# Turning the gathered rows of an expert layer by DMA transposes instead of matmul-engine transposes, from slot 3 on

## What is computed

```python
xn = _layernorm(x, axis=-1)
s = _L0_attn_ref(xn, Wqkv, b_qkv, Wout, b_out)        # attention, (8, 512, 512)
# the feed-forward layer: each token takes the one expert that its router picks
h = jnp.einsum('nd,ehd->enh', x_flat, w_fc)            # 512 -> 2048
a = jnp.square(jnp.where(h >= 0, h, 0.5 * h))
expert_out = jnp.einsum('enh,edh->end', a, w_proj)     # 2048 -> 512
out = jnp.einsum('end,en->nd', expert_out, mask * top_weight[None, :])
g = _silu(out)
x = x + s * g
```

## Time and profile before

| | before |
|---|---|
| median of 3 runs | 1480.56 us (1479.88 to 1480.98) |
| the profiled execution | 1481.51 us, of which the span from first to last instruction is 1479.7 us |
| PE busy | 1384.0 us (94%) |
| DVE, ACT, POOL busy | 923.9, 770.7, 682.5 us |
| DMA, mean | 90 GB/s |

### The profile page before, as it was taken

How to read it: one execution, slowest core, us unless ns; L and a number is a source line. 1 busy time by engine, 2 the same in 40 slices (tenths; PEclk the granted TensorE clock), 3 DMA queues, 4 the chain that set the end, 5 groups by cost and what they waited for, 6 DMA issues and landing times.

```text
span 1479.7 us, 30039 instructions
## 1 busy us (share of the span) xinstructions
PE 1384.0 (94%) x9863; PEld 880.8 (60%) x9863; DVE 923.9 (62%) x2441; ACT 770.7 (52%) x1824; POOL 682.5 (46%) x896
## 2 busy tenths in 40 slices
PE   2889999999999999999689999999999999999995
PEld 1455555655555565555456666666666666666663
DVE  7577777777777777777759745555444555544444
ACT  3478778787777878787736422222222222222221
POOL 0356667465666746566523433333333333323332
PEclk9989999999999999999999999999999999999998
DMA  4425334343534434245346311110011111010100
GB/s 161 144 86 148 125 115 125 110 139 100 171 101 130 128 106 138 89 141 140 107 164 207 115 44 44 44 43 25 23 41 42 39 44 44 30 29 30 36 30 30
DMA packets 84897, 133.45 MB, mean 90 GB/s; under 512 B 14095, under 2 KB 63247, under 8 KB 82576
## 3 DMA queue, kind: packets, MB, share of 16 engines
q1 hardware_dynamic: 75808, 105.70, 23.0%
q0 software_dynamic: 8944, 25.83, 5.6%
HBM read 97.81 MB, written 33.95 MB: 89 GB/s over the span
## 4 chain that ended last, share of the span: by engine, by line
PE 75%; DVE 10%; POOL 6%; ACT 3%; issue 3%; DMA 1%; DVEq 1%; SPq 0%; ACTq 0%; POOLq 0%
PE psY L1126 19%; PE psF L1106 19%; PE psA L352 19%; PE psT L446 7%; PE psA L461 5%; POOL pr L941 4%; PE psS L425 3%; DVE sg L1303 2%; PE psX L1080 1%; POOL route L969 1%; PE psA L409 1%; DVE stat L749 1%; DVE am L636 1%; ACT stage L519 1%; DVE wf L1225 1%
## 5 line engine op out<-in xcount | busy, mean ns | idle before, releaser
L1106 PE MATMUL psF<-xT,wf 128*128 128x256 f16 (+1 forms) x3264 | 368.0, 269 | 0.0
L1126 PE MATMUL psY<-wf,aT 128*128 x1584 | 363.9, 379 | 0.3 <-DVE aT L1270 0.3
L1106 PEld LDWEIGHTS psF<-xT,wf 128*128 x3264 | 312.0, 98 | 63.5
L1344 POOL TENSOR_TENSOR a<-a 128x512 f32<-128x512 f32 (+1 forms) x136 | 153.1, 1126 | 392.1 <-DVE a L1261 390.5
L941 POOL TENSOR_SCALAR pr<-pr,rden 128x128 f32<-128x128 f32 (+3 forms) x512 | 268.4, 542 | 141.9 <-DVE rden L868 140.3
L579 ACT ACTIVATE pr<-pr,mn 128x128 f32<-128x128 f32 (+3 forms) x512 | 281.9, 553 | 0.0
L857 DVE CUSTOM_DVE_ANT_0 pr<-psS,base,nsl 128x128 f32<-128x128 f32 (+3 forms) x512 | 249.6, 543 | 4.2 <-PE psS L425 4.2
L1126 PEld LDWEIGHTS psY<-wf,aT 128*128 128x128 f16 x1584 | 154.5, 98 | 158.5 <-issue 1.0
L446 PE MATMUL psT<-conf,pr 128*128 128x128 f32 x1280 | 205.7, 279 | 18.1 <-POOL pr L941 16.5
L1183 ACT ACTIVATE rl<-psF 128x512 f32<-128x512 f32 (+1 forms) x136 | 79.3, 583 | 263.2 <-PE psF L1106 263.0
L446 PEld LDWEIGHTS psT<-conf,pr 128*128 128x128 f32 x1280 | 157.3, 143 | 81.3 <-POOL pr L941 27.3
(11 more groups left out here) (155 smaller groups left out, 1371.0 us busy)
## 6 DMA issues: line engine op xcount, KB each, us to landing
qk_parts<-pre SPq DMA_DIRECT2D x64, 256.0 KB, 2.8
qs<-qk_parts SPq DMA_DIRECT2D x128, 128.0 KB, 2.7
ks<-qk_parts SPq DMA_DIRECT2D x128, 128.0 KB, 2.7
wst<-in_wf SPq DMA_DIRECT2D x16, 1024.0 KB
wstage<-in_wf SPq DMA_DIRECT2D x32, 512.0 KB, 4.6
xin<-in_x SPq DMA_DIRECT2D x32, 256.0 KB, 4.4
attn_out<-so SPq DMA_DIRECT2D x32, 256.0 KB, 2.0
pt<-in_wqkv SPq DMA_DIRECT2D x4, 768.0 KB, 10.1
```

The costliest lines, as they stand in the source:

```text
L1106: last = nc.tensor.matmul(psF[c % 2][:, k * TT:k * TT + tn], w(e, 2 * hc, hl, kc * 512 + col, P), xT[:, r % 2, x, kc, 0:tn], start=(m == 0 ...
L1126: last = nc.tensor.matmul(psY[r % 2][h][:], aT[:, c % 4, x, k, h * P:(h + 1) * P], w(e, 2 * hc + 1, hl, q * 512, 512), start=(c == 0 and k ...
L1344: nc.gpsimd.tensor_tensor(at, at, at, ALU.mult).then_inc(s["a_ready"], 1)
```

## The change

The rows of slots 3 to 16 are no longer turned by PE. ACT and DVE split the normalised half into its high and low parts token by token, into a new view `xs` of the staging ring (free once the weights are in), and SP then issues eight DMA transposes for each half: two parts by four blocks of 128 by 128 float16, each from `xs` in SBUF to `xT` in SBUF. The first `up` of such a slot waits for the semaphores of these DMAs. Slots 0 to 2 are turned as before. SP issues the transposes in a loop that stands behind all its other work.

```diff
@@ att_sync
         for i in range(QB):
             sp.wait_ge(s_out[i], 16 * (B + 1))
+        ffn["turn"](sp)
@@
+BY_DMA = 3
@@ ffn_block
+    xs = wstage[:, 0, :].bitcast(F16).rearrange("p (h x d) -> p h x d", h=NH, x=2)
+    turned_in = [sem(f"turned_in{i}") for i in range(NH)]
@@
+    def turn(sp):
+        for n in range(BY_DMA, SLOTS):
+            for h in range(halves(n)):
+                sp.wait_ge(s["X_lo"], n * NH + h + 1)
+                sp.wait_ge(s["F_done"], (n - 1) * GR)
+                for x in range(2):
+                    for kc in range(KC):
+                        sp.dma_start_transpose(xT[:, n % 2, x, kc, h * P:(h + 1) * P],
+                                               xs[:, h, x, kc * P:(kc + 1) * P]).then_inc(turned_in[h], 16)
+
+    def rows_turned(eng, n, h):
+        eng.wait_ge(turned_in[h], (n - BY_DMA + 1) * 2 * KC * 16)
@@ up
-            if c == 0:
+            if c == 0 and n < BY_DMA:
                 wait(pe, s["X_lo"], n * NH + halves(n))
+            if c == 0 and n >= BY_DMA:
+                for h in range(halves(n)):
+                    rows_turned(pe, n, h)
@@ step of PE
-                if c in (1, 3) and n >= 0 and ahead and (c - 1) // 2 < halves(n + 1):
+                if c in (1, 3) and n >= 0 and ahead and n + 1 < BY_DMA:
                     xtrans(pe, n + 1, (c - 1) // 2)
@@ turn_hi
+        if n >= BY_DMA:
+            act.wait_ge(s["ln_done"], n * NH + h + 1)
+            if n == BY_DMA:
+                act.wait_ge(s["ws_lo"], len(order))
+            else:
+                rows_turned(act, n - 1, h)
+            nc.scalar.activation(xs[:, h, 0, :], xn[:], ACT.Copy, scale=1024.0).then_inc(s["X_hi"], 1)
+            return
@@ norm
-        wait(dve, s["X_done"], n * NH + h)
+        k = n * NH + h
+        wait(dve, s["X_done"], min(k, BY_DMA * NH))
+        if k > BY_DMA * NH:
+            dve.wait_ge(s["X_hi"], k)
+            dve.wait_ge(s["X_lo"], k)
@@ turn_lo
+        if n >= BY_DMA:
+            stt(out=xs[:, h, 1, :], in0=xn[:], scalar=1024.0, in1=xs[:, h, 0, :],
+                op0=ALU.mult, op1=ALU.subtract).then_inc(s["X_lo"], 1)
+            return
```

More of the change, by code:

```diff
@@ L1361, in ffn_gpsimd @@
         pool.wait_ge(s["out_done"], ((SLOTS - 1) * NH + 1) * 16)
-    return {"sync": load, "pieces": len(order), "xtrans": xtrans, "tensor": ffn_tensor, "split_hi": split_hi,
+    return {"sync": load, "turn": turn, "pieces": len(order), "xtrans": xtrans, "tensor": ffn_tensor, "split_hi": split_hi,
             "turn_hi": turn_hi, "scalar": ffn_scalar, "split_lo": split_lo, "fetch": fetch, "norm": norm,
```

## The result

The changed kernel takes 1558.4 us (median of 4 runs, 1552.7 to 1559.9) against 1480.2 us (1479.5 to 1481.0): a ratio of 1.052, interval 1.049 to 1.054. It is slower by 78 us, where 15 us less were forecast. The profiled execution has a span of 1558.0 us, 78.3 more than that of before.

The account below looks back on a forecast made before the run. PE was taken to bound the second stage; removing its transposes and their wait saves 15.8 us, additions cost nothing, so 1481.51 - 15.8 = 1465.7, adjusted to the runs' median and two more waits: 1465.0 us, range 1463 to 1540.

Parts of the forecast that it names:

- What bounds the kernel, and what goes: Second stage: PE bounds; transposes and their wait go, 1.16 us a slot, 15.8 us in all.
- ACT and DVE: Each half's split, now reading SBUF: +0.04 us on ACT, -0.01 on DVE, new waits costing nothing.
- The deadline: Next slot's first `up`: transposes must land within 10.4 us for the second half, 17.5 us for both.
- L: Time from a DMA transpose's issue to its landing, taken as 2.7 us from SP's stacking DMAs.
- T, the pace: Time from one of SP's DMA transposes to the next, taken as 0.75 us, between 0.43 and 0.9.
- The condition 15T + L under 17.5: Both halves' 16 DMA transposes must land within 17.5 us, before the next slot's first `up`.
- Rival A: Transposes paced over 1 us make PE wait at each slot's first `up`: 1528 at T = 1.31; chance 0.35.
- its signs: Rival A's profile: PE idle once a slot ahead of `up`, released by a DMA, about none for slot 16.
- Rival C: Faster by less: second half late by some tenths, 11 of the 15.8 us come back, 1476; chance 0.04.
- a factor of 2.3 "in hand": SP's issue: a transpose's work for the queue would have to exceed a copy's by over 2.3 to matter.

## Why the prediction was wrong

- **What bounds the kernel, and what goes**: right. All kernels in which PE does not wait lie at 1462 to 1467 us, against a forecast of 1465.0 for this case; span to span the kernel with two DMAs a half gains 1479.7 - 1463.6 = 16.1 us (forecast 15.8).
- **ACT and DVE**: right. The copy takes 621 ns (was 595 from PSUM), the low part 686 (685), and PE waits for neither.

```profile
L1284 DVE SCALAR_TENSOR_TENSOR wstage<-xn,wstage x20: 680/686/693, 957.9 to 1404.6; 128x512 f16<-128x512 f32 x20
```

- **The deadline**: right. 17.5 us for both halves; in the slot shown PE is ready at 1123.68, the first low part at 1106.16, 17.52 apart.
- **L**: 2.7 taken, 2.4 measured. Right enough.
- **T, the pace: this is the step that failed.** I took 0.75 us, "near the lower end", because SP issues plain DMAs every 0.425 us. It measured 1.27 in quiet stretches, 1.365 with the one long issue in the slot shown, and 1.33 on the mean of the 13 full slots. A plain DMA's issue was the wrong row for an instruction of another kind: even plain copies of these blocks took 601 ns, and the transpose doubles that. The condition 15T + L under 17.5 was mine, and with the measured T and L it gives 15 x 1.365 + 2.4 - 17.5 = 5.4 us for the slot in which PE waits 5.55, and 20.0 + 2.4 - 17.5 = 4.9 us on the mean, where 5.03 were measured. The row that I had given to the rival (1.31 us, POOL's pace) was the nearer one, although it comes from another engine's work.
- **Rival A** therefore is what happened, at 1528 in its form with T = 1.31; its signs are there (one wait a slot, ended by the last landing, and none in slot 16). It fell 30 us short, for a term that neither the forecast nor the rivals had: behind each wait of some 5 us the clock is at the lower level for a time, and the next `up` takes 4.09 to 5.30 us in place of 2.62, 2.2 us a slot on the mean. This also took the time out of the range, whose upper end of 1540 was built from waits alone; waits alone would have given 1464 + 65 = 1529. The experiment that keeps PE busy shows it: 19.4 of the 28.7 us come back, and all but 0.6 of the rest is placed. That waits of this kind could be priced by their length alone was an assumption of the range, made without a reason.
- **Rival C** has a slip: it names the second half as the late one and T near 0.99, but its sum, 15 x 0.95 + 4.1 - 17.5, is that of both halves with T = 0.95. It had 0.04 of the chances and did not decide anything.
- **The chance** of the forecast, 0.55, leaned on a factor of 2.3 "in hand" that came from one row of another kind of instruction. With 16 serial instructions against 17.5 us, 1.0 us each was the whole allowance.
- The Trainium skill's figure (page "VectorE: DVE Perf Modes", section "The three transpose paths", 1309 ns for 128 by 128 by DMA) was weighed in the prediction and set aside as possibly a latency. Here the latency is 2.4 us, and the pace 1.27 us, near that figure. But the runs show that the pace is not a price per 128 by 128 block: eight blocks in one instruction take SP 1237 ns too.
- Where the long issues come from (15 of the 216 take over 1.7 us, up to 2.65) was not tried. They are not the transposes' alone: of the 216 plain copies, 8 took 1.1 to 2.1 us against a median of 0.60. They are 0.06 us of the mean pace of 1.33, and without them 15 x 1.27 + 2.4 = 21.5 us are still over the 17.5.

## What to carry to other kernels

Where a change moves work to a DMA queue, count instructions before bytes: the issuing engine's time for each, times their number, against the gap between the data's being ready and the first reader. Put as many blocks as the access pattern allows into one DMA transpose (here 16 instructions became 4 or 2, and a loss of 5% a gain of 1.1%), or turn the data earlier. And price a wait on the matmul engine of some 5 us at more than its length (here 5.03 us of wait and 2.2 us behind it), since the clock behind it is low as well; waits of up to 3.2 us cost only 0.17 us more than their length.

## What the runs showed of the hardware that was not expected

- A DMA transpose costs the issuing SP 1.23 to 1.26 us (medians) whether it moves one 128 by 128 float16 block, four or eight; the landing after the issue is 2.4, 2.5 and 3.1 us. A plain copy of one such block costs 0.60 us.
- After each of the 13 waits of 4.65 to 5.69 us PE ran at the lower level for a time: 24 matmuls took 4.09 to 5.30 us in place of 2.62 (granted clock 0.50 in the slot shown). After waits of 0.3 to 3.2 us they took 2.79 to 2.85 us, at a mean granted clock of 1.00. Matmuls whose results nobody reads, put into the wait, kept the clock at 1.00 and made the kernel 19 us faster.
- 216 DMA transposes among the gathers and scatters of the same slots cost the kernel nothing that showed: turned a slot earlier, the time is 1465.8 us, although the longest gather took 5.4 us to land and not 3.6.
